# Attention scores from fp16 halves, q and k biases by a two-row product, projections one slot earlier, and a reordered prologue

## The chip, the cores and the metric

The kernel runs on one core of a Trainium2 chip (trn2). Its engines work side by side, each through its own list of instructions: TensorE (PE in the profile, its weight loads PEld), VectorE (DVE), ScalarE (ACT), GpSimd (POOL), and SyncE (SP), which issues most DMA loads. They meet by semaphores alone. The metric is the device time of one execution in microseconds, less is better.

## What is computed

Eight sequences of 512 rows and 512 columns go through four layers. The change touches the first two of them. Cut to what matters:

```python
# layer 0, per sequence (its expert is chosen by domain_id)
hidden = gelu(x @ down_W.T + down_b)
hidden = where(valid, hidden @ expert_W[idx].T + expert_b[idx], hidden) + domain_emb[idx]
x = layernorm(hidden @ up_W.T + up_b + x) * ln_gamma + ln_beta
# layer 1
scale, shift = split(silu(sin_emb(timestep)) @ W_ada + b_ada)
x = layernorm(x) * (1 + scale) + shift
q, k, v = x @ Wq + bq, x @ Wk + bk, x @ Wv + bv        # 16 heads of 32
scores = (q / sqrt(32)) @ k.T + attention_bias         # [16, 512, 512]
probs = softmax(where(mask, -inf, scores))
x = x + (probs @ v) @ Wo + bo
# then a feed-forward part, layer 2 (an expert's) and layer 3 (a stencil)
```

All of it is float32. The kernel forms float32 products of whole matrices from fp16 halves: a number is a high half plus a low half, and a product is high x high + low x high + high x low, three fp16 products into one sum (`three`, lines L588 to L590 of the kernel before).

## The kernel before

The program has two passes. The attention pass takes the first 1094 us: a prologue of some 60 us (weights are loaded and split, layer 0 is done for sequence 0), then a loop of seven passes, one per sequence, and the last sequence written out behind it. The feed-forward pass does the rest.

**Slots.** PE's order in a sequence is written out by hand. It is a row of 20 slots, numbered u. A slot of the first 16 stands for four heads (the group g = u // 4) and 128 query rows (j = u % 4). In slot u PE does, in this order: the scores of u (two mask products, L685, for heads 2 and 3, and the "burst" L688: four heads at once, each in its own group of 32 rows of the array, since a head has 32 columns); the last of the four transposes of slot u - 2; what the table BESIDE lists for u; two transposes of slot u - 1; products of probabilities and v (`values`, L702); the third transpose of slot u - 1. A key of BESIDE names a product: ("q", m), ("k", m), ("v", m) are projections of the sequence at hand (q and k for group m, v for 128 rows), "xT", "down", "expert" and "up" are layer 0 of the next sequence, ("R", g) the transpose of the reciprocal row sums. q0, k0, v0 and v1 come ahead of slot 0. Slots 16 to 19 hold the tail, with Wo's product among them.

**Banks.** The scores of a slot fill PSUM banks 0 to 3, one head each, and there is one set of them: slot u + 1's scores can begin only when DVE has taken those of u (semaphore `scored`). Banks 4 to 6 are a ring that the transposes and all keys of BESIDE go through in order; bank 7 holds the context. `claim` lets PE wait until the last user of a bank has been read, and `read_by` says whose semaphore tells that.

**The other engines in a slot.** DVE: four evacuations of scores (L1077, which adds the bias and mask and takes the row's maximum), then what BESIDE has for it (k's evacuation L1039, layer 0's parts), the copies of two transposes (L1092), the context (L1049), and in slots 5, 6, 10 and 11 the layer-norm statistics of two tiles of the next sequence (L967, L969). ACT: four exponentials (L857), two transposes' evacuations (L843), q's evacuation with its bias and scale (L818), v's. POOL adds the mask to the bias tiles that SP loads (L561, the tile called `stage` in the trace). Where a name is shared by several uses of memory the trace shows one of them: q32 is `w_words`, b_ada and the rows of ada are `x`, x1's halves are `hT_hi` and `hT_lo`, W_ada is `stage`.

**Prologue.** Layer 0 and its norm run for sequence 0 with DVE as the chain. PE makes the 8 rows of scale and shift (W_ada, L636), DVE adds b_ada and 1, SP writes them to HBM (L446) and loads those of sequence 0 back onto all partitions as `ada` (L416). Then DVE does the second norm (L999, L1002), PE transposes x1 (L647), and the loop begins. Spin products (L624) fill PE's idle time.

## Time and profile before

| what | value |
|---|---|
| median of 3 runs | 2546.38 us (2546.37 to 2546.72) |
| profiled execution | 2548.05 us, of which the span from first to last instruction is 2546.2 us |
| mean granted clock of TensorE | 0.992 |
| busy share of the span | PE 97%, PEld 48%, DVE 75%, ACT 44%, POOL 38% |
| instructions | PE 14369, DVE 3700, ACT 2160, POOL 829 |

Shares are of the whole span; a stage has its own. A start in the rows is in us from the start of the span, and a group of like instructions in sequence is one row with its count (x8). The bracket at a row's end is the idle time of the engine just ahead of it and what ended it. A row's length includes what overlaps with the next; differences of starts say how long something really held the engine.

### The profile page before, as it was taken

To read this page: it belongs to the slowest core of one execution; us is meant where nothing else is said; L and a number is where in the kernel's file an instruction comes from. 1 tells how busy PE (TensorE), PEld (TensorE's weight loads), DVE (VectorE), ACT (ScalarE), POOL (GpSimd) and SP (SyncE) were. 2 spreads that over 40 slices of the span, in tenths; PEclk is the share of its full clock that TensorE was granted. 3 is DMA by queue.
4 is the path that set the end of the run, shared out by engine and by line. 5 is a ranking of instruction groups with operands and counts; after the bars stand their busy time and mean duration, and the time that the engine had idled before them with its cause. 6 is when DMAs were issued, how large, how long until landed. Compare 5 with 4: busy or idle time off the path is not lost.

```text
span 2546.2 us, 45850 instructions
## 1 busy us (share of the span) xinstructions
PE 2470.9 (97%) x14369; PEld 1223.5 (48%) x14456; DVE 1921.7 (75%) x3700; ACT 1127.6 (44%) x2160; POOL 978.1 (38%) x829
## 2 busy tenths in 40 slices
PE   6999999999999999999999999999999999999996
PEld 4454545455555555544444444444444444444443
DVE  7877777777778685663598688678786886886887
ACT  3676757575758575742223223233222322232331
POOL 1464646464646464410044143242341441432321
PEclk8999999999999999999999999999999999999998
DMA  6445444454544445551232142133222321421340
GB/s 221 143 152 162 150 154 160 147 166 148 158 148 156 150 150 168 163 191 42 79 112 90 61 141 89 56 120 115 83 87 91 108 91 62 141 84 58 123 169 17
DMA packets 150760, 312.29 MB, mean 123 GB/s; under 512 B 16642, under 2 KB 21762, under 8 KB 150546
## 3 DMA queue, kind: packets, MB, share of 16 engines
q1 hardware_dynamic: 141330, 293.01, 35.1%
q10 hardware_dynamic: 9216, 16.78, 1.8%
q8 instruction: 92, 1.51, 0.2%
q14 instruction: 122, 1.00, 0.1%
HBM read 292.75 MB, written 16.81 MB: 122 GB/s over the span
## 4 chain that ended last, share of the span: by engine, by line
PE 53%; DVE 3%; issue 1%; ACT 0%; DVEq 0%; ACTq 0%
PE ffn_bank L1469 17%; PE ffn_bank L1471 17%; PE ffn_bank L1470 17%; PE ffn_bank L1455 1%; PE ffn_bank L1533 1%; PE ffn_bank L1475 1%; DVE g2T_hi L1777 1%; DVE g2T_lo L1778 0%; DVE w_lo L1835 0%; DVE w_hi L1835 0%; PE ffn_bank L1566 0%; DVE stage L1740 0%; ACT g L1611 0%; DVE stage L1721 0%; DVE f L1829 0%
## 5 line engine op out<-in xcount | busy, mean ns | idle before, releaser
L1077 DVE CUSTOM_DVE_ANT_0 w_words<-bank,stage 128x512 f32<-128x512 f32 x512 | 323.7, 686 | 92.7 <-PE bank L688 86.7
L857 ACT ACTIVATE w_words<-w_words,nmax 128x512 f32<-128x512 f32 x512 | 363.4, 714 | 42.2 <-DVE nmax L1077 42.1
L561 POOL TENSOR_TENSOR stage<-stage,mask_add 128x1024 f32<-128x1024 f32 x128 | 272.9, 2143 | 215.3 <-DMA stage<-in_bias 197.6
L1777 DVE CAST g2T_hi<-g 128x512 f16<-128x512 f32 x256 | 179.5, 701 | 221.0 <-ACT g L1611 216.5
L711 PE MATMUL bank<-ident,w_words 128*128 128x128 f32 x2048 | 299.6, 280 | 16.2 <-DVE late L1092 4.7
L711 PEld LDWEIGHTS bank<-ident,w_words 128*128 128x128 f32 x2048 | 222.7, 140 | 175.2 <-issue 83.4
L1778 DVE TENSOR_TENSOR g2T_lo<-g,g2T_hi 128x512 f16<-128x512 f32 x256 | 243.6, 951 | 8.8
L1611 ACT ACTIVATE g<-ffn_bank,bi 128x512 f32<-128x512 f32 x128 | 88.0, 687 | 350.1 <-PE ffn_bank L1471 328.9
L843 ACT ACTIVATE late<-bank 128x512 f32<-128x512 f32 x256 | 151.0, 590 | 151.7 <-PE bank L711 151.5
L1405 POOL TENSOR_TENSOR late<-late,b 128x512 f32<-128x512 f32 x32 | 39.6, 1269 | 464.0 <-DVE f L1809 464.0
L1391 POOL TENSOR_TENSOR stage<-grid,f 128x512 f32<-128x512 f32 x84 | 138.5, 1675 | 200.2 <-DVE f L1680 75.3
L1786 DVE SCALAR_TENSOR_TENSOR wl_lo<-stage,wl_hi 128x1024 f16<-128x1024 f32 x128 | 198.6, 1552 | 5.0 <-ACT wl_hi L1623 5.0
L1469 PE MATMUL ffn_bank<-hT_hi,w_words 128*128 128x512 f16 x512 | 195.3, 381 | 5.7 <-PEq L183 5.7
L1469 PE MATMUL ffn_bank<-wl_hi,g2T_hi 128*128 128x512 f16 x512 | 194.1, 379 | 3.4 <-DVE g2T_lo L1778 3.4
L1469 PE MATMUL ffn_bank<-hT_hi,wl_hi 128*128 128x512 f16 x512 | 194.2, 379 | 1.2 <-DVE hT_lo L1759 1.2
L1470 PE MATMUL ffn_bank<-hT_lo,w_words 128*128 128x512 f16 x512 | 195.2, 381 | 0.0
L1471 PE MATMUL ffn_bank<-hT_hi,w_words 128*128 128x512 f16 x512 | 195.1, 381 | 0.0
L1469 PE MATMUL ffn_bank<-w_hi,g2T_hi 128*128 128x512 f16 x512 | 194.1, 379 | 0.1
L1470 PE MATMUL ffn_bank<-w_lo,g2T_hi 128*128 128x512 f16 x512 | 194.0, 379 | 0.0
L1471 PE MATMUL ffn_bank<-w_hi,g2T_lo 128*128 128x512 f16 x512 | 194.0, 379 | 0.0
L1470 PE MATMUL ffn_bank<-wl_lo,g2T_hi 128*128 128x512 f16 x512 | 194.0, 379 | 0.0
L1471 PE MATMUL ffn_bank<-wl_hi,g2T_lo 128*128 128x512 f16 x512 | 194.0, 379 | 0.0
(277 smaller groups left out, 4886.3 us busy)
## 6 DMA issues: line engine op xcount, KB each, us to landing
stage<-in_bias SPq DMA_DIRECT2D x256, 512.0 KB, 4.3
stage<-in_W_l SPq DMA_DIRECT2D x128, 512.0 KB, 3.3
grid<-in_grids SPq DMA_DIRECT2D x140, 256.0 KB, 3.6
xin<-in_x SPq DMA_DIRECT2D x32, 256.0 KB, 4.0
x_rows<-w_words ACTq DMA_DIRECT2D x32, 256.0 KB, 3.7
late<-x_rows SPq DMA_DIRECT2D x8, 1024.0 KB, 8.7
out<-stage ACTq DMA_DIRECT2D x32, 256.0 KB, 2.0
l_rows<-in_rows SPq DMA_DIRECT2D x8, 768.0 KB, 6.6
```

Of the source, the lines that this page charges most:

```text
L561: pool.tensor_tensor(bias[:, n % NB, :, :], bias[:, n % NB, :, :], mask_add[:, u % T, :].unsqueeze(1).to_broadcast([P, 2, S]), ALU.add).th ...
L711: mm = pe.transpose(bank[:, t * P:(t + 1) * P], tiles[:, 4 * (u % NR) + i, t * P:(t + 1) * P], ident[:, :])
L843: act.activation(pT[:, (u // 2) % 2, i, :, (u % 2) * P:(u % 2 + 1) * P], bank[:, :].rearrange("p (t q) -> p t q", t=T), ACT.Copy).then_inc ...
L857: act.activation(tile, tile, ACT.Exp, scale=-1.0, bias=nmax[:, u % 2, i:i + 1], accum_out=rsum[:, j, h:h + 1]).then_inc(prob_ready, 1)
L1077: dve.tensor_tensor_reduce(tiles[:, 4 * (u % NR) + i, :], bank[:, :], bias[:, half % NB, i % 2, :], -1.0, 3.0e38, ALU.add, ALU.min, nmax[: ...
L1391: pool.tensor_tensor(prod[:, i, :], grid[:, i, :], f[:, t, :], ALU.mult).then_inc(alpha_prod, 1)
L1469: pe.matmul(out, w[0], x[0], start=first, stop=False)
L1470: pe.matmul(out, w[0], x[1], start=False, stop=False)
L1471: return pe.matmul(out, w[1], x[0], start=False, stop=last)
L1777: link(dve.tensor_copy(gT[0][:, n % 4, :], g32[:, n % 2, :]))
L1778: dve.tensor_tensor(gT[1][:, n % 4, :], g32[:, n % 2, :], gT[0][:, n % 4, :], ALU.subtract)\
L1786: dve.scalar_tensor_tensor(out=wl[1][:, k % NW, :], in0=raw[:, k % 2, :], scalar=WS, in1=wl[0][:, k % NW, :], op0=ALU.mult, op1=ALU.subtract)\
```

## The change

1. Scores. q and k are kept as fp16 halves (q16, k16) and a burst is three rounds of four products (high x high, high x low, low x high) in place of one round of four fp32 products.
2. Biases. bq and bk leave the evacuations. POOL makes `qk_b` once: two fp16 rows, high and low half of the scaled bias, and a product of these two rows with `ones` closes the group of each q and k projection.
3. Evacuation. ACT writes the high half of q and of k, then DVE the low half from the same bank. `read_by` for q and k now names DVE's semaphore.
4. BESIDE. q1, k1, q2, k2, q3 and k3 each stand one slot earlier, and v3 two slots later. Slots 7 and 11 have no key any more.
5. q0's products start as each chunk of x1's high half is there; `values` waits for each v apart.
6. Prologue. dom is loaded and clipped first and the expert's weights come ahead of Wq. A dummy Gelu stands early on ACT. Statistics and norms on DVE go tile by tile without a wait between the two steps of one tile (`stats_first`, `norm_first`). b_ada is one row, added by an fp32 product of one row, and ACT takes the rows of ada from PSUM. POOL's adds of bo wait for all four tiles.

```diff
-BESIDE = {0: [("v", 2), ("xT", 0), ("xT", 1)], 1: [("v", 3), ("xT", 2), ("xT", 3)],
+BESIDE = {0: [("v", 2), ("xT", 0), ("xT", 1)], 1: [("xT", 2), ("xT", 3), ("q", 1)],
...
         def read_by(key):
...
-                    "up": (y_ready, T, k), "x1T": (x1T_split, C, k), "q": (q32_ready, C, k),
-                    "k": (k32_ready, C, k), "v": (v32_ready, T, k), "S": (scored, H * T, k),
+                    "up": (y_ready, T, k), "x1T": (x1T_split, C, k), "q": (q_split, C, k),
+                    "k": (k_split, C, k), "v": (v32_ready, T, k), "S": (scored, H * T, k),
...
         @block.sync
...
             for dst, src in VECS[:5]:
                 sp.dma_start(dst, src).then_inc(vec_in, 16)
-            load_weight(2)
             sp.wait_ge(dom_clipped, 1)
             load_expert(slice(0, 1))
+            load_weight(2)
...
         @block.gpsimd
...
+            pool.tensor_scalar(b_scaled, b_raw, WS, None, ALU.mult).then_inc(b_chain, 1)
...
+            pool.tensor_tensor(qk_b[:, :, :], b_raw, b_low, ALU.add).then_inc(b_chain, 1)
+            pool.memset(ones[:, :], 1.0).then_inc(b_chain, 1)
...
+                pool.wait_ge(x1_ready, it * T + T)
                 for t in range(T):
                     pool.wait_ge(x2_ready, it * T + t + 1)
-                    pool.wait_ge(x1_ready, it * T + t + 1)
...
         @block.tensor
...
-                    mm = pe.matmul(psum[6 + i][0:B, :], emb[:, c, :], w_ada[:, c, i * D:(i + 1) * D],
-                                   start=(c == 0), stop=(c == C - 1))
-                mm.then_inc(ada_full, 1)
+                    pe.matmul(psum[6 + i][0:B, :], emb[:, c, :], w_ada[:, c, i * D:(i + 1) * D], start=(c == 0), stop=False)
+                pe.wait_ge(ident_set, 4)
+                pe.matmul(psum[6 + i][0:B, :], ones_row[:, :], b_ada[:, i * D:(i + 1) * D], start=False, stop=True)\
+                    .then_inc(ada_full, 1)
...
                 def project(key):
...
-                        mm = three(bank[:, :], w, x, c == 0, c == C - 1)
+                        mm = three(bank[:, :], w, x, c == 0, c == C - 1 and name == "v")
+                    if name != "v":
+                        if m == 0:
+                            pe.wait_ge(b_chain, 7)
+                        mm = pe.matmul(bank[:, :], qk_b[:, "qk".index(name), m * P:(m + 1) * P], ones[:, :].to_broadcast([2, S]), start=False, stop=True)
...
                 def scores(u):
...
-                    for i in range(4):
-                        rows = slice(HD * i, HD * i + HD)
-                        pe.matmul(psum[i][:, :], q32[rows, g, j * P:(j + 1) * P], k32[rows, g, :],
-                                  start=i < 2, stop=True).then_inc(full[i], 1)
+                    for n, (qs, ks) in enumerate(((0, 0), (0, 1), (1, 0))):
+                        for i in range(4):
+                            rows = slice(HD * i, HD * i + HD)
+                            mm = pe.matmul(psum[i][:, :], q16[qs][rows, g, j * P:(j + 1) * P], k16[ks][rows, g, :],
+                                           start=n == 0 and i < 2, stop=n == 2)
+                            if n == 2:
+                                mm.then_inc(full[i], 1)
...
         @block.scalar
...
+            for i, plus in ((0, 1.0), (1, 0.0)):
+                act.wait_ge(ada_full, i + 1)
+                act.activation(rows[:, i * D:(i + 1) * D], psum[6 + i][0:B, :], ACT.Identity, bias=plus).then_inc(rows_ready, 1)
...
-                        act.activation(q32[:, m, :], bank[:, :], ACT.Identity, scale=1.0 / (WS * math.sqrt(HD)),
-                                       bias=bq[:, m:m + 1]).then_inc(q32_ready, 1)
+                        act.activation(q16[0][:, m, :], bank[:, :], ACT.Copy, scale=Q_SCALE).then_inc(q_hi, 1)
+                    elif name == "k":
+                        bank = arrived(act, it, key)
+                        act.activation(k16[0][:, m, :], bank[:, :], ACT.Copy, scale=1.0 / WS).then_inc(k_hi, 1)
...
         @block.vector
...
-                    if name == "k":
-                        bank = arrived(dve, it, key)
-                        dve.tensor_scalar(k32[:, m, :], bank[:, :], 1.0 / WS, bk[:, m:m + 1], ALU.mult, ALU.add)\
-                            .then_inc(k32_ready, 1)
+                    if name in ("q", "k"):
+                        bank = psum[place(it, key)[0]]
+                        pair, scale, hi, ready = {"q": (q16, Q_SCALE, q_hi, q_split), "k": (k16, 1.0 / WS, k_hi, k_split)}[name]
+                        dve.wait_ge(hi, it * C + m + 1)
+                        dve.scalar_tensor_tensor(out=pair[1][:, m, :], in0=bank[:, :], scalar=scale, in1=pair[0][:, m, :],
+                                                 op0=ALU.mult, op1=ALU.subtract).then_inc(ready, 1)
```

In the rows of instructions below, `hT_hi` and `hT_lo` are x1's halves, `late` is a transpose's copy, `mask_add` the mask. PE in the loop of the kernel before, from the end of k3's projection in slot 11 to slot 12's scores:

```order
L590 MATMUL bank<-hT_hi,wk_lo 128x512
L711 MATMUL bank<-ident,w_words 128x128 x8
L702 MATMUL bank<-late,v 32x256 x8
L711 MATMUL bank<-ident,w_words 128x128 x4
L357 REGISTER_ALU x3
L685 MATMUL bank<-mask_add,ident_bf 128x512
L357 REGISTER_ALU
L685 MATMUL bank<-mask_add,ident_bf 128x512
L688 MATMUL bank<-k,w_words 128x512 x4
```

The same stretch in the changed kernel, where it is the end of slot 10 and slot 11's scores:

```order
L612 MATMUL bank<-hT_hi,wk_lo 128x512
L704 MATMUL bank<-ones,qk_b 128x512
L755 MATMUL bank<-ident,w_words 128x128 x8
L746 MATMUL bank<-late,v 32x256 x8
L755 MATMUL bank<-ident,w_words 128x128 x4
L366 REGISTER_ALU x3
L724 MATMUL bank<-mask_add,ident_bf 128x512
L366 REGISTER_ALU
L724 MATMUL bank<-mask_add,ident_bf 128x512
L728 MATMUL bank<-k_hi,w_words 128x512 x4
L728 MATMUL bank<-k_lo,w_words 128x512 x4
L728 MATMUL bank<-k_hi,w_words 128x512 x4
```

The bias product (L704) has come in behind the projection, the projection stands a slot earlier, and the burst has three rounds.

DVE in slot 10 of the kernel before, behind the evacuation of the scores:

```order
L363 REGISTER_ALU
L1092 COPY late<-bank 128x4x128
L363 REGISTER_ALU
L1092 COPY late<-bank 128x4x128
L1046 REGISTER_ALU
L1049 TENSOR_TENSOR ctx<-bank,rinv_T 128x512
L967 BN_STATS stats<-xin 128x6
L892 REGISTER_ALU
L969 BN_AGGR mv<-stats 128x2
```

and of the changed kernel:

```order
L1096 SCALAR_TENSOR_TENSOR k_lo<-bank,k_hi 128x512
L372 REGISTER_ALU
L1150 COPY late<-bank 128x4x128
L372 REGISTER_ALU
L1150 COPY late<-bank 128x4x128
L1103 REGISTER_ALU
L1106 TENSOR_TENSOR ctx<-bank,rinv_T 128x512
L1018 BN_STATS stats<-xin 128x6
L943 REGISTER_ALU
L1020 BN_AGGR mv<-stats 128x2
```

k3's low half, whose full-precision counterpart L1039 stood in slot 11, has come ahead of slot 10's two copies; a second pair of statistics follows in both.

DVE at the end of slot 2, where g is layer 0's hidden row (its low half is L955, L1006 in the changed kernel). Before:

```order
L953 ISA
L954 CAST ctx<-rinv_T 128x512
L892 REGISTER_ALU
L955 TENSOR_TENSOR ctx<-rinv_T,ctx 128x512
L363 REGISTER_ALU
L1092 COPY late<-bank 128x4x128 x2
```

and changed:

```order
L1004 ISA
L1005 CAST ctx<-rinv_T 128x512
L943 REGISTER_ALU
L1006 TENSOR_TENSOR ctx<-rinv_T,ctx 128x512
L1096 SCALAR_TENSOR_TENSOR k_lo<-bank,k_hi 128x512
L372 REGISTER_ALU
L1150 COPY late<-bank 128x4x128 x2
```

k1's low half stands between g's low half and the two copies.

## Rows read from the trace of the kernel before

**Rows 1.** Windows: PE, PEld, DVE, ACT, POOL busy; PEclk; DMA share; GB/s.
```profile
451.54:580.90 129.36, 126.58 (x929) 68.47 (x941) 97.40 (x223) 87.30 (x197) 71.05 (x74) 1.00 0.49 154
```

**Rows 2.** One line's instructions, L688: durations min, median, max in ns.
```profile
L688 PE MATMUL bank<-k,w_words x1024: 587/640/692, 71.1 to 1066.7; 32*128 32x512 f32 x171
```

**Rows 3.** Timeline of PE in slots 7 to 10 of one sequence.
```profile
511.90 1.14 PE L688 MATMUL bank<-k,w_words 32*128 32x512 f32 x8
...
519.04 1.14 PE L688 MATMUL bank<-k,w_words 32*128 32x512 f32 x8
...
523.59 1.14 PE L688 MATMUL bank<-k,w_words 32*128 32x512 f32 x8
...
526.73 0.63 PE L711 MATMUL bank<-ident,w_words 128*128 128x128 f32 x4 [0.54 <-ACT late L843]
...
529.31 1.14 PE L688 MATMUL bank<-k,w_words 32*128 32x512 f32 x8
530.38 0.66 PE L711 MATMUL bank<-ident,w_words 128*128 128x128 f32 x4
```

**Rows 4.** Timeline of PE in the second part of the program.
```profile
1373.14 1.03 PE L1455 MATMUL ffn_bank<-late,dmat 128*128 128x512 f16 x4
1374.10 0.39 PE L1455 MATMUL ffn_bank<-halo,halo_w 8*128 8x512 f16 x1
1374.41 0.39 PE L1469 MATMUL ffn_bank<-hT_hi,wl_hi 128*128 128x512 f16 x1
```

**Rows 5.** Timeline of PE, end of slot 1 to the start of slot 3.
```profile
473.68 1.25 PE L711 MATMUL bank<-ident,w_words 128*128 128x128 f32 x8 [0.49 <-DVE xT_lo L951]
...
482.04 1.66 PE L711 MATMUL bank<-ident,w_words 128*128 128x128 f32 x12
...
484.06 1.14 PE L688 MATMUL bank<-k,w_words 32*128 32x512 f32 x8
485.43 0.66 PE L711 MATMUL bank<-ident,w_words 128*128 128x128 f32 x4 [0.22 <-DVE late L1092]
```

**Rows 6.** Timeline of all engines, the end of slot 2.
```profile
481.87 2.35 POOL L561 TENSOR_TENSOR stage<-stage,mask_add 128x1024 f32<-128x1024 f32 x1 [0.45 <-DMA stage<-in_bias]
...
482.24 0.69 ACT L818 ACTIVATE w_words<-bank,bq 128x512 f32<-128x512 f32 x1 [0.47 <-PE bank L590]
482.27 2.50 DVE L955 TENSOR_TENSOR ctx<-rinv_T,ctx 128x512 f16<-128x512 f32 x1
```

**Rows 7.** Timeline of DVE in slots 6 to 11.
```profile
513.89 0.69 DVE L1077 CUSTOM_DVE_ANT_0 w_words<-bank,stage 128x512 f32<-128x512 f32 x1 [0.17 <-issue]
...
530.71 0.69 DVE L1077 CUSTOM_DVE_ANT_0 w_words<-bank,stage 128x512 f32<-128x512 f32 x1 [1.61 <-PE bank L688]
...
531.33 0.68 DVE L1077 CUSTOM_DVE_ANT_0 w_words<-bank,stage 128x512 f32<-128x512 f32 x1
...
540.80 0.75 DVE L1039 TENSOR_SCALAR k<-bank,bk 128x512 f32<-128x512 f32 x1
541.47 1.28 DVE L1092 COPY late<-bank 128x512 f32<-128x512 f32 x2
542.67 0.68 DVE L967 BATCH_NORM_STATS2 stats<-xin 128x6 f32<-128x512 f32 x1
...
544.99 0.69 DVE L1077 CUSTOM_DVE_ANT_0 w_words<-bank,stage 128x512 f32<-128x512 f32 x1 [0.39 <-PE bank L688]
```

**Rows 8.** Timeline of all engines in the prologue.
```profile
28.11 8.72 PE L636 MATMUL bank<-stage,emb 128*8 128x512 f32 x16 [2.12 <-DMA x<-in_b_ada]
...
40.58 0.35 SPq L416 DMA_DIRECT2D ada<-ada_rows  x1
...
47.95 0.75 DVE L999 SCALAR_TENSOR_TENSOR xin<-xin,mv,ada 128x512 f32<-128x512 f32 x1 [0.16 <-DVE rstd L83]
...
55.09 1.54 DVE L1002 SCALAR_TENSOR_TENSOR xin<-xin,rstd,ada 128x512 f32<-128x512 f32 x1
```

**Rows 9.** DMA issues from 38 to 45 us: KB each, median us to landing.
```profile
ada<-ada_rows SPq DMA_DIRECT2D x1, 512.0 KB, 3.4
```

More of the change, by code:

```diff
@@ L803, in _ @@
                 l0_part(None, key)
+            act.wait_ge(emb_ready, 2)
+            act.activation(ang[:, 0, 0:1], ang[:, 0, 0:1], ACT.Gelu)
             act.wait_ge(vec_in, 16 * 5)
@@ L832, in sequence @@
                 take(("q", 0))
+                take(("k", 0))
                 take(("v", 0))
@@ L985, in _, with stats_first @@
             weight_lo(2)
-            for name in ("y", "stats0"):
+            def stats_first(ready):
                 for t in range(T):
-                    l0_part(link, None, (name, t))
+                    dve.wait_ge(ready, t + 1)
+                    links[0] += 1
+                    dve.bn_stats(stats[:, t, :], xin[:, t, :]).then_inc(chain, 1)
+                dve.wait_ge(chain, links[0])
+                dve.sem_inc(carrier, 1)
+                for t in range(T):
+                    dve.bn_aggr(mv[:, t, :], stats[:, t, :]).then_inc(stats_ready, 1)
             def rstd_first(which):
@@ L1005, in _ @@
+            for t in range(T):
+                l0_part(link, None, ("y", t))
+            stats_first(y_ready)
             rstd_first(0)
             dve.wait_ge(vec_later_in, 16 * (len(VECS) - 5))
-            for t in range(2):
-                norm_first(0, t)
-            for i in range(2):
-                dve.wait_ge(ada_full, i + 1)
-                dve.tensor_tensor(rows[:, i * D:(i + 1) * D], psum[6 + i][0:B, :], b_ada[:, i * D:(i + 1) * D],
-                                  ALU.add).then_inc(rows_ready, 1)
```

109 lines of the change are left out of this document (73 added, 36 removed), and 3 rows, old and new, of the table BESIDE.

## The prediction, made before the changed kernel ran

> **What bounds the kernel now.** I read the windows first. Seven of the eight sequences run as passes of one loop; one pass lasts 129.36 us with 126.58 us of PE, at a granted clock of 1.00, and DVE, the next engine, is busy for 97.40 us, 75% [rows 1]. So anything that costs PE time costs the kernel time, and a pass holds some 3 us in which PE waits. The timeline of PE shows where. The reader should take the time from one scores burst (L688) to the next as the length of a slot: a slot with a projection beside it lasts 7.14 us (511.90 to 519.04), a bare one 4.55 (519.04 to 523.59), so a projection of 12 products costs 2.59, or 0.216 each; slot 9 lasts 5.72 and has a wait of about 0.70 on ACT in it, of which the row shows 0.54 as idle [rows 3]. Two more waits: about 0.49 on DVE's xT_lo at the end of slot 1, and two of about 0.3 at the start of slot 3. There the burst is followed after 1.37 us (484.06 to 485.43) instead of the usual 1.07 (529.31 to 530.38), and the second, behind those four transposes, I put at the same size [rows 3, 5]. The second half of the program, the feed-forward pass, isn't touched by the change.
>
> The profiled execution took 2548.05 us, 1.67 us above the median of the runs, 2546.38. I sum the differences per pass and put them on the median.
>
> **Scores.** A burst is now 8 fp32 records, from 529.31 to the next start at 530.38: 1.07 us [rows 3]. One record lasts 587 to 692 ns [rows 2]; the shorter and the longer differ by 0.105, which I read as one exposed weight load ahead of the first four. Each record of four 32-row groups runs together, so the burst is two rounds of about 0.52. After the change there are three rounds of fp16 products. With 0.216 for a 512-column fp16 product, a round is that long, and one exposed load and the group's own skew remain: 3 x 0.216 + 0.10 + 0.02 = 0.77. That saves 0.30 per slot, over 16 slots 4.8 us per sequence. Bounds: a burst that exposes 0.105 once more saves 0.20; with a load exposed ahead of each of three rounds and their tails (0.1 more each) it saves nothing. I take 0.30, since two fp32 rounds show just one exposed load. The Trainium skill, "TensorE: Matmul & The Clock Gate", Part 3 (Measured speedup vs the span model), gives 3.07 times for four packed 32-row products of 512 columns, not 4: by that a burst would be an estimated 12 x 0.216 / 3.07 = 0.84, and the sum 128 x 0.07 = 9 us higher. The row of the fp32 burst bears out four groups that start together.
>
> **Biases.** Every q and k projection now ends with a two-row product of 512 columns. Nothing of two rows stands in the trace; the nearest is the halo product of the second half, 8 rows of 512 columns between 128-row products. It starts at 1374.10, and the next one at 1374.41, so 0.31, and its predecessors take 1.03 - 0.07 = 0.96 for four, 0.10 more than 4 x 0.216 [rows 4]. A switch of row form so costs 0.10 on each side: 0.216 + 0.10 + 0.10 = 0.42, and I allow 0.05 more where an fp32 transpose follows (6 of 8). Per sequence 2 x 0.42 + 6 x 0.47 = 3.6 us. Bounds: 0.216 each if nothing is drained (1.7 us), and the same rows give no reason for more than 0.47. "TensorEngine Tiling (Array Packing)", Key Properties, in the Trainium skill says that a change of tiling mode drains the engine; the halo rows agree, with 0.10 on each side.
> PE's content per sequence therefore falls by 4.8 - 3.6 = 1.2 us only.
>
> **What the moved projections do.** Up to now ACT alone read q's bank and DVE alone k's. Now a bank comes free only when DVE has made the low half, after ACT has made the high half (0.69 by L818 [rows 6], DVE 0.66 start to start by L1039 [rows 7]). DVE's queue so stands between a projection and PE's next claim of its bank. By slots, with -0.30 in each of the sixteen:
> - Slots 0 and 1. q1 takes v3's place, and its extra product, with those of q0 and k0, adds 1.4. The wait at the end of slot 1 (0.49, for xT_lo) goes, as 12 products now stand between. -0.6 + 1.4 - 0.5 = +0.3.
> - Slot 2: k1 in q1's place, +0.47 - 0.30 = +0.17, and a new wait. PE's third group of transposes, T(1,2), needs the bank that k1 leaves. Before, ACT left q1's at 482.9 (482.24 + 0.69) and PE ran its 12 transposes without a gap from 482.04 [rows 5, 6]. Now k1's low half stands on DVE behind the subtraction of L955, which the row shows held for 2.50 us, until 484.77, in company with POOL's L561 (481.87 to 484.22) [rows 6]. The low half ends at about 485.4, PE is ready at 483.2: 2.2 us, less by what slots 0 and 1 shift, 2.0. Slot 2: +2.2. Queued behind on DVE are the copies of T(1,0) and T(1,1) and the evacuation of the next scores, which PE awaits in slot 3 anyway.
> - Slots 3 and 4: v3 replaces k1, nothing. The two waits of 0.3 go, as DVE has been waited for already. -0.6 - 0.7 = -1.3.
> - Slot 5: q2 comes in, 2.59 + 0.47 - 0.30 = +2.8.
> - Slots 6 to 8: k2 for q2 (+0.47), k2 out of slot 7 (-2.59), bursts -0.9, and a new wait at slot 8. DVE begins slot 7's scores at 513.89, 1.99 after the burst began at 511.90 [rows 3, 7], since it has two stats with their aggregation in slot 6 (1.9 us, as 542.67 to 544.99 less 0.39 of idling). With k2's low half it begins 0.66 later, at +2.65, and four evacuations of 0.61 (531.33 less 530.71 is 0.62) end at +5.09. Slot 7 is bare for PE, 4.25, so slot 8's burst waits 0.85. Together -2.2.
> - Slots 9 to 14: bursts -1.8; q3 in slot 9 (+3.06), k3 for q3 in slot 10 (+0.47), k3 out of slot 11 (-2.59), and the wait of slot 9 (0.70) goes: -1.6. Against it DVE in slots 10 and 11. Slot 10 on DVE: k3's low half can't start before PE has closed k3 at +4.3 and ACT has made the high half, +5.05; then .66 + 1.20 for two copies (540.80, 541.47, 542.67 [rows 7]) + 0.61 for the context + 1.9 for stats, +9.4, where PE has 7.3. Slot 11 has 2.44 of scores, 1.20 of copies and 1.9 of stats, until +15.0; PE would be at 7.3 + 4.25 = 11.5. Slot 12's burst waits 0.4 for scores of slot 11 (till 11.9), and slot 13's, ready at 16.2, for those of slot 12 (15.0 + 2.44 = 17.5): 1.3, and about 0.7 more is left in slots 13 and 14 before DVE, at 4.0 to 5.1 a slot, has caught up. 2.4 in all, so +0.8.
> - Slot 15 to the end: -0.3.
> Sum: 0.3 + 2.2 - 1.3 + 2.8 - 2.2 + 0.8 - 0.3 = +2.3 us a pass, 16 over seven. The last sequence has none of the next one's work on DVE, so its waits don't grow: -0.5.
>
> **Prologue.** Its end is the row of ada and the norm that uses it (L1002, last at 55.09 + 1.54) [rows 8]. DVE's chain gets shorter: stats and norms in pairs, rows to ACT, and its L1002, 1.54 long in company with POOL's add, would be as short as L999, 0.75, so its eight instructions need 8 x 0.67 = 5.4 us where they took 8.7 (47.95 to 56.63) [rows 8]; 0.67 is the pitch of such an instruction at 540.80 [rows 7]. But ada still has to come. Its products start at 28.11, when b_ada has landed, and last 8.72 for 16 records [rows 8]. Four records more for the bias, at 8.72 / 16 each, are 2.2, so they end at 39.0, not 36.8. From there to the issue of ada's load at 40.58 pass 3.75 us; with the rows on ACT instead of in three steps on DVE I put that at 1 less. The load lands 3.4 after its issue [rows 9]: 39.0 + 2.8 + 3.4 = 45.2. Then 5.4: 50.6 against 56.6. That is -6, with two low halves more on DVE ahead of slot 0's scores -5. Bounds: -1 if b_ada's one-row load lands later or the tables reload, -7 at best. What hides the removed DVE work is this very path. I cost at nothing POOL's seven small instructions for the bias rows and its adds put off until all four tiles are there (POOL has no other work until the first mask adds), the order of SP's loads (expert ahead of Wq, dom first), and q0's products that start on x1's high halves, ahead of 9 products that still need the rest; the Gelu table loaded early, and ACT's extra 0.69 per k, are covered as long as ACT, 87.30 us of a pass [rows 1], stays behind the scores; uncovered, the latter would be 2.8 us a pass.
>
> **Sum:** 16 - 0.5 - 5 = +10.5. 2546.4 + 10.5 = 2557.
>
> **Rivals.**
> - Waits don't grow (0.30). The projections moved a slot ahead give PE work where it waited, and DVE's order works out: for it speaks that DVE is only 75% busy (97.40 of 129.36 [rows 1]); against it, that the load is uneven, two slots in a row with stats. Then 8 x -1.2 - 5 = -15, 2532; with the three old waits gone as well (1.9 a pass) 2519. This is the one on the other side. It decides at 1.5 us of new waits per pass where I count 5.2.
> - The two-row product needs no drain (0.10): 8 x 1.9 = 15 less, 2542.
> - The fp16 rounds expose their weight loads (0.10). One more of 0.105 in 128 bursts gives +13, 2570, all three and no saving +38, 2595. Against it, two fp32 rounds with one load. The Trainium skill, "TensorE: Matmul & The Clock Gate", Part 3 (The mechanism), says that a weight load overlaps products in flight only in another row group, and here each round loads the groups in use; by it this case would be the likely one. The fp32 burst, 1.07 for two rounds, speaks against.
> - The prologue gives nothing, as ada is later by its bias product (0.06): 2562.
> - The forecast (0.44): 2548 to 2566 by itself.
>
> A measurement of this kernel tells 0.2%, 5 us, from no change. Faster: nine tenths of the first rival and half of the second, and little else, 0.34. Same: 0.10 of my own case and the rest of these, 0.16. Slower: 0.50. The range from 2530 to 2570 leaves out a tenth below and a little less above.
>
> **What would show it.** Burst start to next start 0.77 (not 0.87 or more), a bias product 0.42 to 0.47, slot 2 longer by 2.2 with a wait on k_lo (L1096), bursts of slots 8, 12 and 13 that wait for w_words' evacuation (L1135), no wait at slots 1, 3 and 9, a loop pass of 131.6, the first q product 6 us earlier. I'm wrong if slot 2 has no wait, because POOL and DVE don't meet there once the slots shift, or if DVE's low half of k3 comes earlier than I put it.

## The result: 2591 us, slower by 1.7%, and the profile after

The changed kernel took 2591.08 us (median of 4 runs, 2589.31 to 2593.13) against 2546.55 for the kernel before: a ratio of 1.0172, interval 1.0159 to 1.0184. The forecast was 2557, range 2530 to 2570. The sign was right, the size was a quarter of the measured one.

The profiled execution has a span of 2591.3 us, 45.1 more than before. It divides as follows, by starts of PE's bursts (L688 before, L728 after) and of the first and last product of the feed-forward pass:

| stretch | before | after | difference | forecast |
|---|---|---|---|---|
| start to the first burst | 71.14 | 67.08 | -4.1 | -5 |
| first burst to that of the last sequence (seven passes) | 908.91 | 952.39 | +43.5 | +16 |
| last sequence, to the first feed-forward product | 114.82 | 115.26 | +0.4 | -0.5 |
| feed-forward pass, first to last product | 1447.00 | 1452.21 | +5.2 | 0 |

First the windows of the changed kernel, to be held against [rows 1]: one pass of the loop, then slots 2 and 3 of that pass, and slots 2 and 3 of the pass behind it. The columns are those of [rows 1].

```profile
204.70:340.62 135.92, 128.33 (x1014) 67.80 (x1014) 98.23 (x227) 89.33 (x202) 71.33 (x72) 0.99 0.46 147
217.51:228.40 10.89, 8.93 (x56) 4.47 (x56) 7.26 (x14) 8.05 (x15) 5.33 (x3) 1.00 0.30 98
228.40:237.51 9.11, 9.11 (x62) 4.65 (x62) 5.00 (x13) 5.18 (x13) 2.14 (x1) 0.81 0.37 117
353.52:364.51 10.99, 8.93 (x57) 4.49 (x58) 7.36 (x14) 8.05 (x15) 5.08 (x3) 1.00 0.31 96
364.51:371.98 7.47, 7.47 (x62) 4.01 (x63) 4.91 (x13) 5.17 (x13) 1.46 (x1) 1.00 0.44 132
```

The pass has 128.3 us of PE in 135.9, where it had 126.6 in 129.4: PE waits 7.6 us instead of 2.8. And PE's own time went up, though its content went down. The reader sees why in the last column but two of the other rows: in slot 3 of this pass the granted clock was 0.81 and the slot took 9.11 us; in the next pass the same work took 7.47 at 1.00. Five of the seven passes have a slot 3 of 8.5 to 9.1 us. The other two stand behind a slot 2 that is just as long (10.89 and 10.99), so a long slot 2 doesn't lower the clock each time; what decides between the passes is open.

What PE waits for, by PE's waits from 200 to 1000 us, about six passes, in the kernel before (us in total, times, longest) and in the changed one:

```profile
PE bank L711 <- DVE late L1092: 3.7, 12, 0.4
PE bank L711 <- ACT late L843: 3.3, 6, 0.5
PE bank L711 <- DVE xT_lo L951: 2.9, 6, 0.5
```

```profile
PE bank L724 <- DVE nmax L1135: 13.7, 36, 0.9
PE bank L755 <- DVE k_lo L1096: 12.0, 6, 2.1
PE bank L755 <- DVE late L1150: 6.5, 6, 1.1
PE bank L755 <- DVE xT_lo L1002: 5.8, 6, 1.0
```

The evacuation of the scores (L1135, slots 8, 12 and 13), k1's low half (slot 2), a transpose's copy (slot 9) and xT's low half (slot 1) are what grew: 38.0 us here, against 2.9 for xT_lo and 3.7 for the copies before. The last row is the wait that I let vanish; it doubled. The bursts of slots 8, 12 and 13 come 0.9, 0.9 and 1.5 us later than behind a bare slot of 4.24.

The prices of the new instructions were forecast closely. PE in slot 6, its burst and the end of k2's projection:

```profile
252.28 0.40 PE L728 MATMUL bank<-k_hi,w_words 32*128 32x512 f16 x4
252.51 0.39 PE L728 MATMUL bank<-k_lo,w_words 32*128 32x512 f16 x4
252.72 0.39 PE L728 MATMUL bank<-k_hi,w_words 32*128 32x512 f16 x4
253.04 0.66 PE L755 MATMUL bank<-ident,w_words 128*128 128x128 f32 x4
...
255.91 0.38 PE L612 MATMUL bank<-hT_hi,wk_lo 128*128 128x512 f16 x1
256.22 0.39 PE L704 MATMUL bank<-ones,qk_b 2*128 2x512 f16 x1
256.53 1.09 PE L755 MATMUL bank<-ident,w_words 128*128 128x128 f32 x8
```

A burst takes 0.76 from its start to the next (252.28 to 253.04), forecast 0.77, and the bare slot 8 went from 4.55 to 4.24. The bias product starts 0.31 behind the last fp16 product and is followed after 0.31, so 0.41 more than without it; slot 6 with its projection went from 7.14 to 7.30, which is 0.46 for the product less 0.31. The Trainium skill, "TensorE: Matmul & The Clock Gate", Part 3 (Measured speedup vs the span model), has 3.07 times for four packed 32-row products; here 12 products of 0.216 in 0.76 make 3.4. Its statement in the same part (The mechanism), that a weight load overlaps products only of another row group, isn't borne out: three rounds in the same four groups start 0.23 and 0.21 apart, no more than the products themselves take, and the loads of the second round (PEld, from 252.29) run while the first round's products do.

### The profile page after: what moved, and what is told of

Same layout as the page of the kernel before. It is cut to its first block, busy times and chain, and to the rows that moved or that the text cites. A ratio compares the mean times of both kernels' runs of the same rounds, so it can differ in the third digit from the quotient of the medians.

```text
span 2591.3 us, 47121 instructions
## 1 busy us (share of the span) xinstructions
PE 2482.1 (96%) x15036; PEld 1217.3 (47%) x15036; DVE 1946.1 (75%) x3728; ACT 1145.1 (44%) x2195; POOL 997.5 (38%) x837
## 3 DMA queue, kind: packets, MB, share of 16 engines
q1 hardware_dynamic: 141036, 292.98, 34.3%
## 4 chain that ended last, share of the span: by engine, by line
PE 48%; DVE 5%; issue 2%; ACT 1%; DVEq 0%; ACTq 0%
PE ffn_bank L1527 15%; PE ffn_bank L1529 15%; PE ffn_bank L1528 15%; PE ffn_bank L1513 2%; DVE g2T_hi L1835 1%; DVE g2T_lo L1836 1%; PE ffn_bank L1591 1%; PE ffn_bank L1533 1%; DVE stats L1720 1%; PE ffn_bank L1624 0%; ACT g L1669 0%; DVE w_hi L1893 0%; DVE stage L1798 0%; DVE f L1735 0%; DVE f L1738 0%
## 5 line engine op out<-in xcount | busy, mean ns | idle before, releaser
L1135 DVE CUSTOM_DVE_ANT_0 w_words<-bank,stage 128x512 f32<-128x512 f32 x512 | 323.8, 686 | 67.9 <-PE bank L728 50.8
```

The lines of the kernel that those rows point to most:

```text
L1135: dve.tensor_tensor_reduce(tiles[:, 4 * (u % NR) + i, :], bank[:, :], bias[:, half % NB, i % 2, :], -1.0, 3.0e38, ALU.add, ALU.min, nmax[: ...
```

## The experiments

All were timed beside the kernel before on the same chip, whose medians were 2547.13 (first four), 2546.94 (next four), 2546.95 (next four) and 2547.94 (last two). Differences between kernels are those of their medians, across chips too, where the kernel before differs by at most 1.4 us. Times of slots are from one profiled execution each. "The stretch of the feed-forward pass" is first to last product, as in the table. Times of slots are from start to start of bursts.

### 1. The changed kernel with the old table

```diff
-BESIDE = {0: [("v", 2), ("xT", 0), ("xT", 1)], 1: [("xT", 2), ("xT", 3), ("q", 1)],
+BESIDE = {0: [("v", 2), ("xT", 0), ("xT", 1)], 1: [("v", 3), ("xT", 2), ("xT", 3)],
...
```

> The changed kernel with the BESIDE table of before, all else as changed. Theory (the waits come from the projections moved a slot earlier: k1's low half behind g's in slot 2, q3 and the mask add of POOL in slot 9, and the granted clock that falls behind slot 2's wait): no wait of 2 us in slot 2, granted clock 1.00 in slot 3, a loop pass of about 128.5 to 130 us, 2532 to 2545 in all. Rival (the two-step evacuation and the bias products cost it, wherever they stand): a pass stays above 134, 2580 or more. The 5 us that the untouched feed-forward pass lost should stay if they hang on the number of instructions ahead of it on DVE, which is that of the changed kernel.

2582.33 us (2578.66 to 2583.98), ratio 1.0134 (1.0117 to 1.0151); a pass takes 133.6 to 135.7 us after the first. The theory as I wrote it fell: slot 2 still takes 11.16, slot 3 7.9 to 9.6. Its waits from 200 to 1000 us say why:

```profile
PE bank L755 <- DVE w_words L1096: 15.3, 12, 2.4
PE bank L755 <- ACT late L894: 7.7, 12, 0.8
```

`w_words` written by L1096 is q's low half; six of the twelve waits, of some 2.3 us each, are those of slot 2. The second row is a transpose's evacuation by ACT, which had 3.3 us in six waits before (L843). With the old table q1 stands in slot 2, and since the change DVE must read q's bank too. So the wait in slot 2 doesn't need k1 there. Any low half behind g's does it. In the kernel before, ACT alone freed q1's bank. The feed-forward stretch was 1451.07, as in the changed kernel.

### 2. The table alone, on the kernel before

```diff
-BESIDE = {0: [("v", 2), ("xT", 0), ("xT", 1)], 1: [("v", 3), ("xT", 2), ("xT", 3)],
+BESIDE = {0: [("v", 2), ("xT", 0), ("xT", 1)], 1: [("xT", 2), ("xT", 3), ("q", 1)],
...
+                        for key in beside(it, u):
+                            if i == (4 if key[0] in ("q", "k") else DVE_AFTER.get(u, 4)):
```

> The kernel before with the new BESIDE table alone (and the rule that q and k are taken at step 3 or 4 of a slot, and values that wait for each v apart). Scores stay fp32, biases stay in the evacuations, q is read by ACT alone. Theory: slot 2 waits for k1 on DVE behind g's low half as in the changed kernel, and slots 7, 9 and 11 to 12 wait, a pass of 133 to 137 us, 2570 to 2600. Rival (the evacuation in two steps makes the waits): a pass within 1 us of 129.4, 2540 to 2555.

2600.60 us (2597.69 to 2601.30), ratio 1.0206 (1.0189 to 1.0223), a pass of 133.1 to 135.1 us after the first. The move alone makes it slow: slot 2 11.26 in most passes, slot 3 7.8 to 9.4, slot 9 8.3. Experiments 1 and 2 together say that either edit suffices to put a DVE-read bank into slot 2; they don't add. The surprise is the feed-forward stretch, 1463.36, 16 us more than before with not a word of it changed. PE's waits there, and the place:

```profile
PE ffn_bank L1474 <- issue: 13.2, 6, 2.6
```

```profile
1480.70 0.38 PE L1473 MATMUL ffn_bank<-hT_lo,w_words 128*128 128x512 f16 x1
1483.16 0.39 PE L1474 MATMUL ffn_bank<-hT_hi,w_words 128*128 128x512 f16 x1 [2.08 <-issue]
```

PE stands still for 2.1 us between two products of one group, waiting for nothing that the waits show, once in each of six passes of the loop. The profile's DMA view has a queue that it calls "instruction", q8 here. In each of the six places one 16 KB packet of it starts within the last 0.5 us before the stop or the first 0.7 us of it, the first between 1480.8 and 1481.0. In the feed-forward pass it moved 66 packets, where it moved 12 before.

### 3. Without the bias products

```diff
-                        mm = pe.matmul(bank[:, :], qk_b[:, "qk".index(name), m * P:(m + 1) * P], ones[:, :].to_broadcast([2, S]), start=False, stop=True)
```

> The changed kernel without the 64 bias products: q and k get no bias (left out of the computation). Theory: 0.42 to 0.47 of PE time each, of which what stands in slots that wait for DVE is given back as longer waits: 15 to 25 us faster than the changed kernel, 2566 to 2576. Rival (a switch of row form costs much more than the records show): over 35 us faster.

2580.69 us, 10.4 less than the changed kernel, below the forecast of 15 to 25: 0.16 for each of 64 products whose PE time is 0.41 to 0.46. In the profiled run only two passes, not five, have a slow slot 3, worth some 4 us of it, so the products themselves gave still less. Slot 1 grew from 8.0 to between 8.3 and 8.7, slot 7 from 5.18 to 5.59 and slot 11 from 5.11 to 5.46 as slots 6 and 10 shrank from 7.30 to 7.04 and 6.83. Where DVE sets the pace, PE time that is taken away comes back as a wait.

### 4. The prologue alone

> The kernel before with the changed prologue alone (order of loads, early Gelu, statistics and norms in pairs, rows of ada by ACT and a one-row product, POOL's adds after all tiles). Theory: the first product of q starts 4 to 6 us earlier, 2540 to 2543 in all. Rival (it delays what comes behind, or moves the feed-forward pass's instructions so that this loses time): 2546 or more.

The edit is part 6 of the change, on the kernel before. 2541.88 us (10 runs, 2539.71 to 2544.30), ratio 0.9980 (0.9970 to 0.9989): faster, as forecast, and the fastest of all kernels here. The first product of q starts 4.1 us earlier and so does the first burst (67.07 instead of 71.14); 1.8 us of the profiled gain lie in the feed-forward pass (1445.25), whose code is the same.

### 5. k1's low half ahead of g's

```diff
-                        for key in beside(it, u):
+                        for key in (reversed(beside(it, u)) if u == 2 else beside(it, u)):
```

> The changed kernel with one edit: in slot 2 DVE takes k1's low half before g's, not behind it. Theory (slot 2's wait of 2 us is DVE's queue behind g's low half, which meets POOL's mask add, and the granted clock falls in slot 3 because of that wait): the wait in slot 2 shrinks to 0.5 to 1.0 us, some of it comes back in slot 3 where the copies and the expert's input now stand behind g's low half; the granted clock of slot 3 is 1.00 in all passes; 1.5 to 2.5 us a pass less than the changed kernel, 2573 to 2581. Rival (k1's bank is late for another reason, ACT's high half): slot 2 keeps its wait, 2588 or more.

2574.70 us (2574.13 to 2575.91), 16.4 less, as forecast. Slot 2 takes 9.41 instead of 10.89, with a wait of 0.48, and slot 3 7.58 to 7.70 at clock 1.00 in all passes. So it is DVE's order that makes k1's low half late, not ACT's high half.

### 6. A mixed table, and 7. without k's bias

```diff
+          2: [("down",), ("v", 3)], 3: [("expert",), ("k", 1)], 4: [("up", 0), ("up", 1)],
+          5: [("R", 0), ("up", 2), ("up", 3)], 6: [("q", 2)], 7: [("k", 2)], 9: [("R", 1)], 10: [("q", 3)],
```

> The changed kernel with q1 in slot 1, v3 in slot 2 and all other projections where they were before the change. So no low half of q or k stands on DVE in slot 2. Theory: no wait of 2 us in slot 2, clock 1.00 in slot 3, slot 9 at 5.7; there remain the waits that the table of before had in slots 6, 7, 11 and 12 with the two-step evacuation (about 2.5 a pass); a pass of 129.5 to 131, 2545 to 2555. Rival (PE waits for the two-step evacuation wherever it stands, and the clock falls with any of it): a pass of 133 or more, 2575 or more.

> As the mixed table, and without the bias products of k (32 of 64). k's bias adds the same number to all scores of a row, which the softmax takes out again, so nothing of the result is left out but k's bias itself. Theory: 32 products of 0.42 to 0.47 less, part of it returned as waits for DVE: 8 to 14 us less than the mixed table, 2533 to 2545. Rival: PE waits for DVE anyway, under 4 us less.

2567.67 us (2566.42 to 2568.77) and 2561.27 (2560.21 to 2562.84). The mixed table missed its forecast of 2545 to 2555, and the run without k's bias its 2533 to 2545. The named waits went (slot 2 8.36, slot 9 5.72, slot 3 at clock 1.00), but a pass is still 131.8 to 132.6 us, where I expected 129.5 to 131: slot 6 takes 7.63 and slot 7 7.98, where content and the forecast bias give 7.30, and slot 11 7.98. PE waits there 0.30 for q2's low half and 0.64 each for k2's and k3's. So the two-step evacuation costs 0.1 us in slot 10 (7.41), 0.3 in slot 6 and 0.7 in slots 7 and 11; this I had counted at nothing unless in slots 2, 6 and 10. Leaving k's bias out gains 6.4 us, 0.20 for each of 32 products, below the forecast of 8 to 14: again less than half of their PE time.

### 8. 64 instructions more on DVE, ahead of the work

```diff
+            for _ in range(64):
+                dve.sem_inc(carrier, 1)
             dve.wait_ge(dom_in, 16)
```

> The changed kernel with 64 instructions more at the start of DVE's program, each raising a semaphore that nobody waits for, at a time when DVE waits for its first load. Nothing is computed by them. Theory (the 5 us that the untouched feed-forward pass lost are DVE's stops of some 1 to 1.5 us between two instructions once a pass of its loop, which depend on where its instructions lie): the stops move to another place or go, and the feed-forward pass is 3 to 6 us shorter, or longer if they land in a worse place. Rival (they come from the memory layout or from DMA traffic): the feed-forward pass as in the changed kernel, within 1 us.

The total is 2591.99 us, since the 64 instructions delay the first burst by 4.2 us (71.31). But the feed-forward stretch is 1447.76 instead of 1452.21. In the changed kernel DVE stops for 1.45 us between g2T_hi and g2T_lo, two instructions that have nothing to wait for, and PE waits for the second; the rows are of that place:

```profile
1490.86 0.69 DVE L1836 TENSOR_TENSOR g2T_lo<-g,g2T_hi 128x512 f16<-128x512 f32 x1 [1.45 <-issue]
...
1503.83 0.39 PE L1527 MATMUL ffn_bank<-w_hi,g2T_hi 128*128 128x512 f16 x1 [1.43 <-DVE g2T_lo L1836]
```

PE's waits for this tile in the feed-forward pass, in the changed kernel and in the run with 64 instructions more:

```profile
PE ffn_bank L1527 <- DVE g2T_lo L1836: 8.9, 13, 1.4
```

```profile
PE ffn_bank L1529 <- DVE g2T_lo L1838: 3.1, 9, 0.4
```

Nothing else was changed, so where DVE's instructions lie decides about these stops. PE's waits behind them, of 0.9 to 1.4 us, come at the same point of each of six passes of that loop. When the pass begins doesn't matter: experiments 3, 9 and 11, which leave DVE's program alone, have 1451.9 to 1452.2 us for it, though it begins at 1121, 1103 and 1129 us instead of 1135.

### 9. POOL's mask adds cut short

```diff
-                    pool.tensor_tensor(bias[:, n % NB, :, :], bias[:, n % NB, :, :],
-                                       mask_add[:, u % T, :].unsqueeze(1).to_broadcast([P, 2, S]), ALU.add).then_inc(masked, 1)
+                    pool.tensor_tensor(bias[:, n % NB, :, 0:1], bias[:, n % NB, :, 0:1],
+                                       mask_add[:, u % T, 0:1].unsqueeze(1).to_broadcast([P, 2, 1]), ALU.add).then_inc(masked, 1)
```

> The changed kernel with POOL's mask add (L583) on one column of each tile in place of 512: the key mask is left out for heads 0 and 1 of each group. The semaphores stay. Theory (g's low half in slot 2, 2.5 us, and the spread of the reciprocals in slot 9, 1.66 us, are long because POOL's add runs beside them; the one makes slot 2's wait and with it the fall of the clock, the other most of slot 9's): g's low half 0.69, spread 0.43, slot 2 1.7 to 2.0 us shorter, slot 3 at 7.47 in all passes, slot 9 about 1.2 shorter; 3 to 4.5 us a pass, 2558 to 2572. Rival (DVE has too much in those slots with or without POOL): under 1 us a pass, 2584 or more.

2562.90 us (2561.63 to 2564.75), 28.2 less. Slots 2, 3 and 9 of one pass:

```profile
210.97:220.37 9.40, 8.92 (x56) 4.46 (x56) 5.56 (x14) 7.45 (x13) 0.19 (x1) 1.00 0.37 112
220.37:227.85 7.48, 7.48 (x63) 4.00 (x63) 4.91 (x13) 5.66 (x15) 0.19 (x1) 1.00 0.42 128
259.33:267.55 8.22, 7.86 (x64) 4.15 (x64) 6.16 (x15) 7.31 (x19) 5.22 (x5) 1.00 0.75 247
```

Slot 2 9.40 with 5.56 of DVE (it was 7.26), slot 3 at clock 1.00 and 7.48, slot 9 8.22 instead of 9.21. The two long instructions of DVE are in slot 2 and ahead of slot 9's transposes, and both lie beside an add of POOL. The first was as long in the kernel before [rows 6], where no bank that PE wanted stood behind it; the second became long with the change:

```profile
223.83 2.29 POOL L583 TENSOR_TENSOR stage<-stage,mask_add 128x1024 f32<-128x1024 f32 x1 [3.28 <-DMA stage<-in_bias]
...
224.16 2.50 DVE L1006 TENSOR_TENSOR ctx<-rinv_T,ctx 128x512 f16<-128x512 f32 x1
...
226.59 0.68 DVE L1096 SCALAR_TENSOR_TENSOR k_lo<-bank,k_hi 128x512 f16<-128x512 f32 x1
...
227.41 0.63 PE L755 MATMUL bank<-ident,w_words 128*128 128x128 f32 x4 [1.97 <-DVE k_lo L1096]
```

```profile
402.29 2.14 POOL L583 TENSOR_TENSOR stage<-stage,mask_add 128x1024 f32<-128x1024 f32 x1
...
403.06 1.66 DVE L1142 COPY rinv_x<-rinv 128x512 f32<-128x512 f32 x1
...
405.37 0.66 PE L755 MATMUL bank<-ident,w_words 128*128 128x128 f32 x4 [1.08 <-DVE late L1150]
```

g's low half, 0.69 when alone, took 2.50, and behind it k1's low half let PE wait 1.97. In two of the seven passes it is g's high half, the cast ahead of it, that meets the add, which then starts at 359.63, and slot 2 is as long:

```profile
359.70 2.33 DVE L1005 CAST ctx<-rinv_T 128x512 f16<-128x512 f32 x1 [2.55 <-ACT rinv_T L819]
```

The spread of the reciprocals, 0.43 when alone, took 1.66, and behind it the copies let PE wait 1.08. In the kernel before, the add was over when the spread began:

```profile
520.32 2.16 POOL L561 TENSOR_TENSOR stage<-stage,mask_add 128x1024 f32<-128x1024 f32 x1
...
523.18 0.43 DVE L1084 COPY rinv_x<-rinv 128x512 f32<-128x512 f32 x1
```

In all these pairs DVE's instruction ends 0.3 to 0.6 us behind POOL's add, a little less than it takes alone, as if it had waited for the add to end. "GPSIMD Engine Reference", 1. Specifications, in the Trainium skill says that GpSimd shares its SBUF interfaces with VectorE, with contention for DVE instructions that have two SBUF inputs or run in a two-port mode. g's low half has two SBUF inputs and agrees; the cast and the spread have one, and no row here names their mode.

### 10. The table alone, with 64 spin products more on PE

```diff
-            SPINS = {("xT", 0): 64, ("down",): 38, ("expert",): 50, ("up", 0): 26}
+            SPINS = {("xT", 0): 128, ("down",): 38, ("expert",): 50, ("up", 0): 26}
```

> The kernel before with the new table, as in the run of the move alone, and 64 spin products more in the prologue, where PE waits for its first load. Theory (the 13 us in which PE of that run stood still between two products of the feed-forward loop, six times 2.2 us, come from where its instructions lie): they go or move, and the feed-forward pass is 10 to 15 us shorter, 2584 to 2592. Rival (memory, DMA or the clock): the same six stops, 2597 or more.

2581.33 us (2580.48 to 2583.10), 19.3 less than experiment 2 and a little below the forecast. The feed-forward stretch fell by 16.5, from 1463.36 to 1446.83, and PE's six stops are gone. The "instruction" queue still moved 67 packets there, so their number alone isn't what stops PE. That a stop is PE waiting for such a packet is likely from their starts, but not shown.

### 11. Spin products in slot 2

```diff
+                    if u == 2:
+                        spin(7, 28)
                     if 0 < u <= NQ:
                         turn(u - 1, 2)
```

> The changed kernel with 28 spin products (1.6 us, into the context's bank, which is idle then) in slot 2 just ahead of T(1,2), where PE waits 1.97 us. Theory (the granted clock falls in slot 3 because PE stood still in slot 2): slot 2 as long as before within 0.2, granted clock 1.00 in slot 3 and 7.47 us in all seven passes, 6 to 9 us faster, 2582 to 2585. Rival (the clock falls for another reason, or the spins lengthen the wait): slot 3 still at 8.4 to 9.1 in most passes, 2590 or more.

2587.12 us (2586.08 to 2588.40), 4.0 less than the changed kernel, a little short of the forecast. Slots 2 and 3 of the pass that corresponds to the first window above:

```profile
217.07:227.96 10.89, 10.49 (x84) 6.09 (x84) 7.26 (x14) 8.04 (x15) 5.51 (x3) 1.00 0.32 98
227.96:235.44 7.48, 7.48 (x63) 4.02 (x63) 4.92 (x13) 5.18 (x13) 1.52 (x1) 1.00 0.41 137
```

Slot 2 lasts as long as it did, with PE busy for 10.49 instead of 8.93, and slot 3 takes 7.47 or 7.48 us in all seven passes. So PE's idle time in slot 2 is what lets the clock fall. The Trainium skill, "TensorE: Matmul & The Clock Gate", Part 1, has an idle array at 1.2 GHz and a busy one at 2.4; the granted clock of 0.81 over slot 3 is a mixture of the two, with products of 512 columns 0.43 us apart at first and 0.22 apart from 232.15 on. Of the 7.5 us that slot 3 gave back, 3 went into two passes whose last stretch took 36.7 and 36.9 instead of 34.8 to 35.5. There PE stands still ahead of the next q0's first product, another stop of the kind of experiment 2:

```profile
733.79 0.39 PE L686 MATMUL bank<-hT_hi,wq_hi 128*128 128x512 f16 x1 [1.73 <-issue]
```

Another 0.9 went into slot 2 of the last sequence (7.71 instead of 6.82), where the spin products stand too and PE had nothing to wait for.

### 12. The new prologue, with ACT's scaling a slot later

```diff
-ACT_L0 = {8: (("scale0", 0), ("scale0", 1)), 9: (("scale0", 2), ("scale0", 3)),
+ACT_L0 = {8: (("scale0", 0), ("scale0", 1)), 10: (("scale0", 2), ("scale0", 3)),
```

> The kernel before with the changed prologue, and ACT's scaling of tiles 2 and 3 of the next sequence taken in slot 10, not 9. Theory: in slot 9 PE waits 0.70 us for a transpose's evacuation that stands behind this scaling on ACT; in slot 10 a projection covers it: slot 9 at 5.02, 4 to 5 us faster than with the prologue alone, 2536 to 2539. Rival (the wait only moves to slot 10 or 11, where POOL's gain and DVE's statistics come later): 2540 or more.

2552.61 us (2550.34 to 2554.82), ratio 1.0023 (1.0014 to 1.0033): a miss. Slot 9 stayed at 5.72, so the scaling wasn't what made PE wait there, and slot 13 grew from 5.08 to 5.9. It is the meeting of experiment 9 again. With the scaling later, three mask adds of POOL run from 279.39 to 285.71, and the spread of the reciprocals lies beside the last of them:

```profile
284.45 1.55 DVE L1097 COPY rinv_x<-rinv 128x512 f32<-128x512 f32 x1
...
286.65 0.66 PE L714 MATMUL bank<-ident,w_words 128*128 128x128 f32 x4 [0.68 <-DVE late L1105]
```

It takes 0.43 in the prologue's own run (experiment 4), and 1.55 to 1.57 here in slot 13 of every sequence.

### 13 and 14. POOL waits for g's low half

```diff
+                    if u == 3 and not is_final(it):
+                        pool.wait_ge(g_split, it + 2)
                     pool.wait_ge(bias_in[n % NB], (it * USES[n % NB] + n // NB + 1) * 16)
```

> The changed kernel; POOL waits for the low half of g before it adds the mask to the tile of slot 3. All of the computation is done. Theory (what makes slot 2 long is that POOL's add and g's low half run side by side): g's low half 0.69, slot 2 at 9.4 to 9.6, granted clock of slot 3 1.00, slot 3 up to 0.5 longer for the later add; 2.0 to 2.7 us a pass, 2572 to 2578. Rival (POOL's amount of work, or the add only moves and lengthens the copies behind it as much): 2586 or more.

> The kernel before with the changed prologue; POOL waits for the low half of g in the same way. Theory: slots 2 and 3 hold 0.3 to 0.8 us of wait a pass by this meeting; what is gained there comes back in part as slot 3's scores that wait for the later add: 0 to 4 us less than the prologue alone, 2538 to 2542. Rival: the later add costs more than the meeting, 2543 or more.

On the changed kernel: 2573.77 us (2572.85 to 2575.56), 17.3 less, with all of POOL's work done. The same place as above:

```profile
222.91 0.69 DVE L1008 TENSOR_TENSOR ctx<-rinv_T,ctx 128x512 f16<-128x512 f32 x1
...
223.77 4.23 POOL L585 TENSOR_TENSOR stage<-stage,mask_add 128x1024 f32<-128x1024 f32 x2 [8.61 <-DVE ctx L1008]
...
223.84 0.69 DVE L1098 SCALAR_TENSOR_TENSOR k_lo<-bank,k_hi 128x512 f16<-128x512 f32 x1 [0.23 <-ACT k_hi L871]
...
224.67 0.63 PE L757 MATMUL bank<-ident,w_words 128*128 128x128 f32 x4 [0.48 <-DVE k_lo L1098]
```

The add has moved behind g's low half, which takes 0.69, PE waits 0.48 where it waited 1.97, slot 2 takes 9.41 and slot 3 7.48 in all passes. In slot 2 it is the meeting that counts, not POOL's amount of work. Slot 9 stays at 9.22, as nothing was done about its meeting. On the new prologue: 2543.55 us, ratio 0.9981 (0.9972 to 0.9991), no different from the prologue alone (0.9980), and past the forecast of 2538 to 2542. Slot 3 there takes 8.45 in all passes, where it took 7.79 to 8.73.

## Why the prediction was right in sign and wrong in size

**What held.** The burst (0.76 for 0.77), the bias product (0.41 to 0.46 for 0.42 to 0.47), slot 2 (+2.1 for +2.2, with the wait for L1096 that I named), slot 5 (+2.75 for +2.8), slots 6 to 8 (-2.1 for -2.2), slots 3 and 4 as long as the clock is full (-1.2 for -1.3). In slots 10 to 14 DVE is behind by the forecast amount: -1.1, where the steps for them give -1.2. Rivals: the waits did grow, the two-row product does switch, the fp16 rounds expose one load, and the prologue gained.

**What failed, per pass.** The step "Sum: ... = +2.3 us a pass" measured +6.4 (135.8 against 129.4, mean of the second to seventh pass). Four terms of it were wrong.
- The clock. The step on slots 3 and 4 took products at full speed. Behind a wait of 1.97 us PE had the lower level for part of slot 3, +1.0 to +1.6 in five of seven passes. I had the wait and didn't ask what it does to the clock; experiment 11 shows the link. In all 7.5 us.
- "The wait of slot 9 (0.70) goes: -1.6." Slot 9 takes 9.21 where the terms give 7.8: +1.4. Slots 7 and 8 together are 2.3 us shorter, so that the spread of the reciprocals at their end now meets POOL's add. About 1.0 of it goes with the add (8.22 in experiment 9); the 0.4 that stays is PE's wait for q3's low half (0.36 there).
- "The wait at the end of slot 1 (0.49, for xT_lo) goes." It doubled:

```profile
215.24 1.91 PE L755 MATMUL bank<-ident,w_words 128*128 128x128 f32 x12 [0.99 <-DVE xT_lo L1002]
```

  xT2 and xT3 stand ahead of q1 now, and ACT and DVE come to them only behind step 3 of the slot (ACT at 213.88, DVE at 214.49), so 12 products in between gain nothing. +0.5.
- Slot 15 to the end, with the products of q0 and k0, is +1.1 for +0.6. Without the bias products (experiment 3) it takes 34.3 where the kernel before took 34.0, so these two cost 0.9 as forecast, and the rest didn't get shorter; why is open.

**What failed elsewhere.** "The second half of the program ... isn't touched by the change": +5.2 us, DVE's stops (experiments 8 and 10). The prologue's -5 measured -4.1; in the eleven other profiles with the new prologue and nothing put ahead of it the first burst comes at 65.1 to 68.7 us, so one profile is good to 2 us. x1's norm ends at 50.9, where I had 50.6, but not by the path that I gave. I let ada's load set the start of the norm (39.0 + 2.8 + 3.4 = 45.2). Its load was issued at 39.89 and landed 3.4 later, at 43.3, since the products of its rows ended at 37.4 and not at 39.0; the norm began at 45.54 behind DVE's own chain of statistics and `rstd`. That the two times agree is luck; the eight instructions in 5.4 us came as forecast. q0's first product starts at 55.16, 5.1 earlier than before; from there to the first burst it takes 11.9 instead of 10.9 us, as the bias products of q0 and k0 stand there. The first row of ada, its load, the start of the norm and its last pair, and q0's first product:

```profile
32.97 0.59 ACT L857 ACTIVATE x<-bank 8x512 f32<-8x512 f32 x1 [1.39 <-PE bank L660]
...
39.89 0.35 SPq L426 DMA_DIRECT2D ada<-ada_rows  x1
...
45.54 1.42 DVE L1058 SCALAR_TENSOR_TENSOR xin<-xin,mv,ada 128x512 f32<-128x512 f32 x2 [0.16 <-DVE rstd L83]
...
49.52 1.41 DVE L1063 SCALAR_TENSOR_TENSOR xin<-xin,rstd,ada 128x512 f32<-128x512 f32 x2
...
55.16 0.39 PE L686 MATMUL bank<-hT_hi,wq_hi 128*128 128x512 f16 x1 [0.84 <-DVE hT_lo L1024]
```

The last sequence was +0.4 for -0.5.

One sum of the first rival was wrong too: by the prediction's own terms its total is zero at some 3.7 us of new waits a pass (2.3 a pass with 5.2 of waits, -5.5 outside the passes), not at 1.5. Here the waits were above both.

The excess of 34.6 us over the forecast of 10.5 is then: seven passes 27.5, of them 7.5 by the clock, 10 by slot 9, 3.5 each by slots 0 to 1 and by the last stretch, the rest spread; the feed-forward pass 5.2; prologue and last sequence 1.8. For slots 2 and 9, the clock and the feed-forward pass experiments show the cause; for slots 0 to 1 it is read from the rows alone.

**What the change costs by part.** The parts don't add up, since the move (experiment 2) and the two-step evacuation (experiment 1) each make slot 2 wait. Best shown is: prologue -5, of which 4 lie ahead of the first burst; everything else, with the old table, +40 (experiment 1 against 4); without slot 2's wait and slot 9's, still +26 (experiment 6 against 4), 6 of it in the feed-forward pass. What fp16 scores give PE, 5.0 us a sequence (16 times 0.31), is taken by the bias products (3.6) and by a DVE that reads every projection's bank.

## What to carry to other kernels

An engine at 75% can set the pace: look at its queue slot by slot, at what a bank's release stands behind, before PE work is counted as gained. When a second engine joins the readers of a buffer, its whole queue joins the path of whoever claims that buffer next. Where GpSimd and VectorE work beside each other, one semaphore that keeps one long add out of the way can be worth more (17 us here) than the arithmetic saved (8 x 1.4 = 11 us), but only where PE waits behind the meeting: on the kernel with the new prologue alone the same semaphore gained nothing. And a wait that opens on TensorE should be costed with the clock behind it.

## What the runs showed that I had not expected

The feed-forward pass, the same code in all runs, took 1445.25 to 1463.36 us. Its length follows where the instructions of DVE and PE lie: 64 more on DVE took 4.4 us away, 64 more on PE 16.5. Most of the stops show as idle time until "issue", in the middle of a row of like instructions, at the same point of each pass of a loop. A difference of under 1% between two versions of a long program can be this alone.
